# Router columns merged into expert 0's gate product, and the expert ranking moved and spread over VectorE

## What is computed

```python
logits = x @ router_w                          # (256, 32)
scores = sigmoid(logits)
grouped = (scores + router_bias).reshape(T, 8, 4)
group_scores = top_k(grouped, 2).sum(-1)
masked = grouped in the 4 best groups, else 0
top_k_index = top_k(masked, 8)
tkw = scores[top_k_index] / sum * 2.5
routed = sum over the 8 experts of tkw * ((silu(x @ w_gate) * (x @ w_up)) @ w_down)
shared = (silu(x @ sw_gate) * (x @ sw_up)) @ sw_down     # hidden width 512
return routed + shared
```

## Time and profile before

| | us |
|---|---|
| median of 3 runs | 532.67 |
| lowest and highest run | 532.51, 533.3 |
| the profiled execution | 532.38 |
| span of that execution | 530.3 |
| TensorE busy (matmuls) | 520.7 |
| VectorE busy | 389.1 |
| ScalarE busy | 304.3 |
| GpSimd busy | 29.4 |

### The profile page before, as it was taken

One profiled execution on the slowest core, in us unless ns is written; L12 is line 12 of the kernel. 1 busy time (PEld: TensorE's weight loads), 2 busy tenths in 40 slices (PEclk: granted clock), 3 DMA queues, 4 the chain that ended last, 5 costly groups with the idle time before them and its releaser, 6 DMA issues.

```text
span 530.3 us, 9657 instructions
## 1 busy us (share of the span) xinstructions
PE 520.7 (98%) x3454; PEld 469.0 (88%) x3454; DVE 389.1 (73%) x616; ACT 304.3 (57%) x470; POOL 29.4 (6%) x48
## 2 busy tenths in 40 slices
PE   9999999999989999989999999999999999999997
PEld 7988888888669989879989999999999999999997
DVE  6777555557788988776987777768677776767675
ACT  5665587753476776637546465554646465554631
POOL 1000000000632131010000000000000000000000
PEclk9999999999999999999999999999999999999999
DMA  8775624455412232516355646464554646455521
GB/s 286 289 231 175 209 99 155 162 159 157 127 35 78 86 136 90 199 41 237 121 183 173 203 157 222 143 225 163 193 189 167 204 161 223 146 215 171 185 71 40
DMA packets 19459, 86.24 MB, mean 163 GB/s; under 512 B 2160, under 2 KB 2416, under 8 KB 19312
## 3 DMA queue, kind: packets, MB, share of 16 engines
q1 hardware_dynamic: 19440, 85.99, 47.9%
HBM read 85.46 MB, written 0.52 MB: 162 GB/s over the span
## 4 chain that ended last, share of the span: by engine, by line
PE 92%; DVE 5%; ACT 2%; issue 1%; POOL 0%; ACTq 0%; DVEq 0%; POOLq 0%
PE bank L936 33%; PE bank L429 16%; PE bank L433 16%; PE bank L432 16%; PE bank L437 2%; PE bank L501 1%; PE bank L438 1%; PE bank L439 1%; PE bank L573 1%; DVE w_lo L282 1%; PE bank L715 1%; PE bank L735 1%; PE bank L696 1%; ACT operands L305 1%; PE bank L455 1%
## 5 line engine op out<-in xcount | busy, mean ns | idle before, releaser
L277 ACT CAST w_hi<-raw 128x768 fp32r<-128x768 f32 (+3 forms) x158 | 158.9, 1040 | 96.6 <-PE bank L936 82.8
L282 DVE TENSOR_TENSOR w_lo<-raw,w_hi 128x1280 fp32r<-128x1280 f32 (+3 forms) x156 | 182.7, 1213 | 13.5 <-ACT w_hi L277 11.4
L429 PE MATMUL bank<-w_hi,operands 128*128 128x512 f32 (+1 forms) x322 | 126.1, 392 | 1.2 <-DVE operands L330 1.0
L433 PE MATMUL bank<-w_hi,operands 128*128 128x512 f32 (+1 forms) x322 | 124.0, 385 | 0.0
L432 PE MATMUL bank<-w_lo,operands 128*128 128x512 f32 (+1 forms) x322 | 123.8, 385 | 0.0
L936 PE MATMUL bank<-xt_hi,w_lo 128*128 128x256 f32 x512 | 108.6, 283 | 0.0
L936 PE MATMUL bank<-xt_hi,w_hi 128*128 128x256 f32 x512 | 108.4, 283 | 0.0
L936 PE MATMUL bank<-xt_lo,w_hi 128*128 128x256 f32 x512 | 108.3, 283 | 0.0
L936 PEld LDWEIGHTS bank<-xt_hi,w_hi 128*128 128x128 f32 x512 | 83.7, 190 | 2.6
L936 PEld LDWEIGHTS bank<-xt_hi,w_lo 128*128 128x128 f32 x512 | 81.7, 190 | 0.0
L936 PEld LDWEIGHTS bank<-xt_lo,w_hi 128*128 128x128 f32 x512 | 81.7, 190 | 0.0
(11 more groups left out here) (182 smaller groups left out, 565.4 us busy)
## 6 DMA issues: line engine op xcount, KB each, us to landing
raw<-w_exp_dram SPq DMA_DIRECT2D x34, 896.0 KB, 4.7
raw<-w_exp_dram SPq DMA_DIRECT2D x34, 640.0 KB, 5.6
raw<-ctx_t_dram SPq DMA_DIRECT2D x16, 512.0 KB, 4.6
raw<-ctx_n_dram SPq DMA_DIRECT2D x16, 512.0 KB, 4.1
raw<-w_mla_dram SPq DMA_DIRECT2D x8, 512.0 KB, 3.6
raw<-w_mla_dram SPq DMA_DIRECT2D x8, 448.0 KB, 3.9
raw<-wq_dram SPq DMA_DIRECT2D x4, 256.0 KB, 5.4
raw<-wk_dram SPq DMA_DIRECT2D x2, 512.0 KB, 7.3
```

The source lines that it names most:

```text
L277: act.copy(w_hi[:, t.slot, at:at + n], raw[:, t.slot, at:at + n]).then_inc(hi_split[k], 1)
L282: eng.tensor_tensor(w_lo[:, t.slot, at:at + n], raw[:, t.slot, at:at + n], w_hi[:, t.slot, at:at + n].bitcast(F32), ALU.subtract) \
L429: ins = pe.matmul(o, a[0], b[0], start=start, stop=False)
L433: return pe.matmul(o, a[1], b[0], start=False, stop=stop)
```

## The change

It takes the router's columns from `smalls` and stores them behind each chunk of expert 0's gate columns in a separate array `w_first` (piece 0 of expert 0 grows from 1280 to 1408 columns, the slot from 3072 to 3200). Expert 0's gate product has 288 columns instead of 256, the last 32 being logits, tokens down. Its up product goes to bank 2 + h. ScalarE copies the logits out and takes the sigmoid of 128 x 64 values, with no transposes. TensorE, ScalarE and VectorE get new orders. The router's own split, matmuls and score transposes go. `expert_lo(2)`, which stood behind `expert_add(1)`, now stands inside the ranking, and `expert_add(0)` behind it. The core of the diff, first SyncE and TensorE (in the code `expert_add(0, s)` and the like with j = 0 are expert s; with j = 1, expert 2 + s):

```diff
+FIRST_SIZES = (1408, 1024, 768)
...
+            load(Tile(0, T_E), w_first, FIRST_SIZES)
+            load(Tile(0, T_E + 1), w_exp[0], E_SIZES)
...
+            def first_gate(h, split, told=None):
+                t = Tile(0, T_E)
+                n = I + E
+                for c in range(NC):
...
+                    ins = product(bank[4 + 2 * h][:, 0:n], (xt_hi[:, c, half(h)], xt_lo[:, c, half(h)]),
+                                  wcols(t, c * n, n), c == 0, c == NC - 1, told if c == 0 else None)
+                ins.then_inc(bank_full[4 + 2 * h], 1)
...
-            expert_rows(0, 0, 4, told=used[1], split=V_LN3)
-            expert_rows(1, 0, 5, midway=lambda: transpose_half(xn, 1, 0, xn_ready, 6))
-            expert_rows(0, 1, 6, split=V_LN3 + 2)
-            expert_rows(1, 1, 7, told=used[2])
-            transpose_hidden(0)
+            first_gate(0, V_LN3, told=used[1])
+            first_up(0)
+            second_rows(0, midway=lambda: transpose_half(xn, 1, 0, xn_ready, 6))
+            first_gate(1, V_LN3 + 2)
+            first_up(1)
+            second_rows(1, told=used[2], midway=lambda: transpose_hidden(0))
...
-            pe.wait_ge(rw_split, 1)
-            for c in range(NC):
-                ins = product(bank[6][0:E, 0:T], (rw_hi[:, c, :], rw_lo[:, c, :]),
-                              (xt_hi[:, c, :], xt_lo[:, c, :]), c == 0, c == NC - 1)
-            ins.then_inc(bank_full[6], 1)
-            transpose_hidden(1)
-            down(0, 0, told=used[2])
-            pe.wait_ge(ev_lo, V_H + 1)
-            pe.wait_ge(sigmoid_ready, 1)
-            for h in range(2):
-                ins = pe.transpose(bank[7][:, h * E:h * E + E], score_t[:, half(h)], ident[0:E, 0:E])
-            ins.then_inc(bank_full[7], 1)
+            pe.wait_ge(logits_copied, 2)
+            down(0, 0, told=used[2])
+            transpose_hidden(1)
             gate_up(0, 2, told=used[1])
-            pe.wait_ge(score_taken, 1)
             down(0, 1, told=used[2])
```

ScalarE's order:

```diff
             rows_silu(1, 0)
             rows_silu(0, 1)
+            for h in range(2):
+                act.copy(logits[:, h * E:h * E + E], bank[4 + 2 * h][:, I:I + E]).then_inc(logits_copied, 1)
             split_hi(act, Tile(0, T_E + 2), 0, E_SIZES)
+            out_hi(act, 2, F23["h_t"], h_hi[:, 0, :], 512)
             rows_silu(1, 1)
...
+            split_hi(act, Tile(0, T_E + 2), 2, E_SIZES)
+            act.wait_ge(logits_copied, 2)
+            act.activation(score, logits, ACT.Sigmoid).then_inc(sigmoid_ready, 1)
+            out_hi(act, 3, F23["h_t"], h_hi[:, 1, :], 512)
             split_hi(act, Tile(0, T_E + 3), 0, E_SIZES)
```

VectorE's order; the `out_lo` of bank 3 stands behind line 1632, the splits of expert 3 behind line 1653:

```diff
             rows_hidden(0, 1)
+            out_lo(dve, 2, V_H, h_hi[:, 0, :], h_lo[:, 0, :], 512)
             split_lo(dve, Tile(0, T_E + 2), 0, E_SIZES)
             rows_hidden(1, 1)
-            out_lo(dve, 0, V_H, h_hi[:, 0, :], h_lo[:, 0, :], 512)
             split_lo(dve, Tile(0, T_E + 2), 2, E_SIZES)
-            out_lo(dve, 1, V_H + 1, h_hi[:, 1, :], h_lo[:, 1, :], 512)
...
-            dve.wait_ge(bank_full[7], F7["score"])
-            dve.tensor_copy(score, bank[7][:, 0:2 * E]).then_inc(score_taken, 1)
-            for k in (0, 2):
-                split_lo(dve, Tile(0, T_E + 3), k, E_SIZES)
-            split_lo(dve, Tile(0, T_E + 2), 1, E_SIZES)
-            expert_add(0, 0)
+            dve.wait_ge(sigmoid_ready, 1)
...
-            expert_product(1, 0)
+            out_lo(dve, 3, V_H + 1, h_hi[:, 1, :], h_lo[:, 1, :], 512)
...
+            for k in (0, 2):
+                split_lo(dve, Tile(0, T_E + 3), k, E_SIZES)
+            split_lo(dve, Tile(0, T_E + 2), 1, E_SIZES)
+            expert_product(1, 0)
             for h in range(2):
                 m = masked[:, h * E:h * E + E]
                 then(dve.max(top8[:, h * TOP:h * TOP + TOP], m))
                 then(dve.match_replace(replaced[:, h * E:h * E + E], top8[:, h * TOP:h * TOP + TOP], m, TAKEN))
+            expert_lo(1, 0)
+            expert_add(0, 0)
             then(dve.tensor_tensor(picked, replaced, masked, ALU.not_equal))
...
             expert_add(0, 1)
-            expert_lo(1, 0)
             expert_splits(1, 0)
             expert_add(1, 0)
```

More of the change, by code:

```diff
@@ L60 @@
 T_E = T_M + PAIRS
-OFF = (0, 1280, 2304)
-SLOT = 3072
+OFF = (0, 1408, 2432)
+SLOT = 3200
 X_SIZES = (1024, 1024)
@@ L68 @@
 E_SIZES = (1280, 1024, 768)
-C_MASK, C_COS, C_SIN, C_RW, C_BIAS, C_GQ, C_GKV, C_TIE = 0, 256, 512, 768, 896, 960, 1152, 1280
+FIRST_SIZES = (1408, 1024, 768)
+C_MASK, C_COS, C_SIN, C_BIAS, C_GQ, C_GKV, C_TIE = 0, 256, 512, 768, 832, 1024, 1152
 C_END = C_TIE + 2 * GROUPS * GROUPS
-F01 = dict(ln1=1, s_even=2, s_new=6, pt_even=7, ot=11, ln2=12, rope=13, y=14, ln3=15, h_t=16, moe=16)
-F23 = dict(q=1, s_odd=2, pt_new=6, pt_odd=7, ot=11, qkv=12, rope=13, scores=14, pt=15, ln3=30, moe=30)
+F01 = dict(ln1=1, s_even=2, s_new=6, pt_even=7, ot=11, ln2=12, rope=13, y=14, ln3=15, moe=15)
+F23 = dict(q=1, s_odd=2, pt_new=6, pt_odd=7, ot=11, qkv=12, rope=13, scores=14, pt=15, ln3=30, up=31, h_t=32, moe=32)
 F45 = dict(ln1=1, k=2, v=3, wo=4, ln2=5, c=6)
@@ L81 @@
 F67 = dict(pv=1, c=2, rows=11)
-F6 = dict(v=3, router=12, moe=13)
-F7 = dict(qk=3, score=12, moe=13)
+F6 = dict(v=3, moe=12)
+F7 = dict(qk=3, moe=12)
 V_LN1, V_Q, V_K, V_V, V_PT, V_OT, V_LN2, V_C, V_M0 = 1, 5, 7, 9, 11, 29, 33, 37, 41
@@ L108, in free, with perceiver_layer @@
         return self.number - 1 if k < 2 else self.number + (-1 - T_E)
-def perceiver_layer(nc, x, small, wq, wk, wv, wo, ctx_t, ctx_n, w_qkv, w_rope, w_mla, w_exp, out):
+def perceiver_layer(nc, x, small, wq, wk, wv, wo, ctx_t, ctx_n, w_qkv, w_rope, w_mla, w_first, w_exp, out):
     with ExitStack() as ctx:
@@ L212, in perceiver_layer @@
         h_row = scores[:, 1, 1024:2048].rearrange("p (r n) -> p r n", r=2)
-        score_t = scores[0:E, 1, 3200:3200 + T]
         def route(at, n):
             return scores[:, 1, 2048 + at:2048 + at + n]
+        logits, score = route(1152, 2 * E), route(0, 2 * E)
         x_loaded = [sem(f"x_loaded{h}") for h in range(2)]
@@ L409, in _ @@
                     load(Tile(j, T_M + s), w_mla[bass.ds(j * 2 + s, 1)].squeeze(0), M_SIZES)
-            for s in range(2):
-                load(Tile(0, T_E + s), w_exp[s], E_SIZES)
+            load(Tile(0, T_E), w_first, FIRST_SIZES)
+            load(Tile(0, T_E + 1), w_exp[0], E_SIZES)
             with sp.Fori(0, NE // 2 - 1) as j:
                 for s in range(2, 4):
-                    load(Tile(j, T_E + s), w_exp[bass.ds(j * 2 + s, 1)].squeeze(0), E_SIZES)
+                    load(Tile(j, T_E + s), w_exp[bass.ds(j * 2 + (s - 1), 1)].squeeze(0), E_SIZES)
             for k, (h, at, n) in enumerate(((0, 0, 512), (1, 0, 256), (1, 256, 256))):
@@ L892, in _, with first_up, second_rows @@
             out_pair(last, last=True, halves=(1,), heads=(1,))
-            def expert_rows(s, h, b, told=None, split=None, midway=None):
-                t = Tile(0, T_E + s)
+            def first_gate(h, split, told=None):
+                t = Tile(0, T_E)
+                n = I + E
+                for c in range(NC):
+                    if h == c == 0:
+                        ready(t, 0)
+                    if c % 2 == 0:
+                        pe.wait_ge(ev_lo, split + c // 2)
+                    ins = product(bank[4 + 2 * h][:, 0:n], (xt_hi[:, c, half(h)], xt_lo[:, c, half(h)]),
+                                  wcols(t, c * n, n), c == 0, c == NC - 1, told if c == 0 else None)
+                ins.then_inc(bank_full[4 + 2 * h], 1)
+            def first_up(h):
+                t = Tile(0, T_E)
+                for c in range(NC):
+                    if h == 0 and c == 1:
+                        ready(t, 2)
+                    at = OFF[2] + (c - 1) * I if c else NC * (I + E)
+                    ins = product(bank[2 + h][:, 0:I], (xt_hi[:, c, half(h)], xt_lo[:, c, half(h)]),
+                                  wcols(t, at, I), c == 0, c == NC - 1)
+                    if h == 1 and c == 0:
+                        ins.then_inc(used[0], 1)
+                ins.then_inc(bank_full[2 + h], 1)
+            def second_rows(h, told=None, midway=None):
+                t = Tile(0, T_E + 1)
                 for u in range(2):
@@ L903, in expert_rows @@
                             ready(t, k)
-                        if split is not None and u == 0 and c % 2 == 0:
-                            pe.wait_ge(ev_lo, split + c // 2)
                         at = (u * NC + c) * I if k == 0 else OFF[2] + (c - 1) * I
-                        ins = product(bank[b][:, u * I:u * I + I], (xt_hi[:, c, half(h)], xt_lo[:, c, half(h)]),
+                        ins = product(bank[5 + 2 * h][:, u * I:u * I + I], (xt_hi[:, c, half(h)], xt_lo[:, c, half(h)]),
                                       wcols(t, at, I), c == 0, c == NC - 1, told if u == c == 0 else None)
@@ L1167, in _ @@
                 pair_step(j, 2)
[L1168 removed]
+            pair_step(0, PAIRS - 3, FIRST_SIZES)
```

(7 more changed lines are left out.)

43 lines of the change are left out of this document (15 added, 28 removed).

## The result

| | before | after |
|---|---|---|
| median of all 10 runs of each, taken in turn | 532.9 | 534.52 |
| lowest and highest run | 532.51, 533.3 | 533.45, 535.42 |
| the profiled execution | 532.38 | 533.45 |
| span of that execution | 530.3 | 531.7 |

The ratio is 1.0028, 95% interval 1.002 to 1.0036. The change makes the kernel slower by 1.6 us by the medians (1.5 by the ratio), where I had forecast 533.0 and no change that can be measured; 534.52 also lies above the upper end of my range, 534.2.

The account below looks back on a forecast made before the run. TensorE bounds the kernel, but VectorE has no reserve from 260.50 to 269.55: gate_up(3) starts 1.41 us earlier, yet a new 2.0 us wait makes gate_up(4) about 0.3 later. 532.38 + 0.3 = 532.7, by the median 533.0; range 531.6 to 534.2.

Parts of the forecast that it names:

- What bounds: From 278 us TensorE alone sets the time; from 260.50 to 269.55 VectorE has no reserve, busy 8.50 of 9.05 us.
- the sum from 240.81 to gate_up(4): Experts: gate_up(3) starts 1.41 us earlier, at 259.12; piece 0 of expert 4 is ready 10.49 later; about +0.3 at gate_up(4).
- the price of 288 columns: Expert 0's gate product: each matmul takes 0.1337 us, on a line between 0.120 for 256 columns and 0.229 for 512.
- the wait of some 0.2 at down(0): TensorE before down(0): a new wait of 0.1 us for the low part of the turned hidden values.
- VectorE's 2.5 us of idle time: VectorE before expert_lo(2): idle 2.4 us, 259.8 to 262.17, until ScalarE has written the high part.
- the wait of 1.93 us: TensorE before gate_up(4): stands 2.0 us until VectorE has split expert 4's piece 0.
- The 128 more columns of piece 0: zero: Head pairs: about 0.1 us each on ScalarE and VectorE, covered, so zero; 0.2 if the cover were gone.
- The clock falls in the new wait: Slower rival: the 2.0 us wait brings the slow pace back for gate_up(4), 3 us or more, 536; chance 0.03.
- The sum is 532.38 + 0.3: Total: 532.7 for an execution like the profiled one, which was 0.29 below the median, so 533.0.
- The gain survives: Faster rival: expert 4's piece 0 is split by 267.6, so -1.94 us, 530.7 by the median; chance 0.11.
- gate_up(3) comes later: Slower rival: time lost between 240.81 and 259.12, at down(0) behind ScalarE's cast, reaches the end, 534.2; chance 0.10.

Follow-up runs that it names:

- the trace with 12 additions: Kernel before with 12 additions of 128x128 on VectorE in front of the splits that hold expert 4's piece 0; 538.27 us, ratio 1.01.
- the one with the split moved: Changed kernel with only VectorE's split of expert 0's piece 0 moved behind the step of the next head pair; 533.21 us, ratio 1.0007.
- The two repairs: Changed kernel with expert_lo(2) back behind expert_add(1), 531.33 us; the same with VectorE's split of expert 0's piece 0 behind the next head pair's step, 530.74.
- the best version: Changed kernel with expert_lo(2) back behind expert_add(1) and VectorE's split of expert 0's piece 0 behind the next head pair's step; 530.74 us, ratio 0.9959.

## Why the prediction was wrong, step by step

**What bounds, and the sum from 240.81 to gate_up(4): right.** TensorE's times, the price of 288 columns (243.41 - 241.82 = 1.59 for 12, so 0.133 each, forecast 0.134), the wait of some 0.2 at down(0) (forecast 0.1), VectorE's 2.5 us of idle time (2.4), the wait of 1.93 us (2.0): all as worked out, to 0.1. In the Trainium skill, TensorE: Matmul & The Clock Gate, section Back-to-back issue gap, the isolated gap between two matmuls at full clock is N / 2.4 + 2.5 ns, which gives an estimate of 122.5 for 288 columns; the measured 133 decides, and the line between this kernel's own 256 and 512 columns was nearer. gate_up(4) and what follows loses 0.38 us (an offset of 1.01 at 241.82 and of 276.71 - 275.32 = 1.39 at down(3)) where I had +0.3.

**"The 128 more columns of piece 0: zero": wrong, +0.46 us.** This is the first step that failed. I costed the columns at nothing because TensorE's busy tenths stand at 9 among the head pairs. A tenth of 9 in slices of 13 us hides a wait of 0.5 us, and above all it says nothing of slack: it does not tell whether the next thing on TensorE waits for VectorE. The row to read was VectorE's queue: which instruction stands behind this split, and who waits for it. I had also priced 0.1 each for ScalarE and VectorE in case the cover was gone, and left out the transfer ahead of them, which with 0.39 in the two traces shown, and 0.21 by the means of five, was the largest of the three.

**"The clock falls in the new wait": chance 0.03, and it happened in 12 of 16 executions.** This is the second. I had forecast the wait, 2.0 us, and named what it could do; against it I had only that the clock held in the stretch with the wait of before, which was 0.25 us. A short wait is no evidence for a long one, and the longest of that trace behind the start, 1.25 us at 158.94, is none either. The size was off the other way. I took the pace of the kernel's first matmuls for a whole gate_up and wrote 3 us or more. At the low clock two matmuls of 256 columns do take 0.43 us (275.15 to 275.58 in the trace with 12 additions) instead of 0.24, but the low stretch ends after 3.4 us and holds 14 to 19 matmul records, not 48: it costs 1.2 to 1.5 by the traces. Between the medians of the two kinds of executions lie 0.8 us in the changed kernel (534.63 against 533.79) and 1.1 in the one with the split moved.

**"The sum is 532.38 + 0.3":** two small terms were missing. The device time less the span is 2.05 to 2.06 us in the seven traces with the arrangement of before and 1.79 to 1.81 in the five that hold the change, 0.26 less. I did not look for the reason. And the profiled execution was not 0.29 below the median, as by the runs shown, but 0.42 to 0.52 below the medians of the four longer sets of runs (532.80 to 532.90).

**Together.** 532.86 + 0.46 + 0.38 - 0.26 = 533.4 for the changed kernel at full clock; its four runs lie at 533.45 to 533.83, median 533.79. With 1.2 to 1.5 for the clock it is 534.6 to 534.9 for the others, measured 534.14 to 535.42. The two repairs come out of the same terms. With the low part moved back gate_up(4) to down(3) is 1.82 us earlier against the stretch's end than before, so 532.86 + 0.46 - 1.82 - 0.26 = 531.24 (measured 531.33); with the split moved as well, 0.22 below the price of before instead of 0.46 above it, 530.56 (530.74). Up to 0.4 us of a total stays unexplained, less than the times of the kernel before scatter (532.33 to 533.66).

**The rivals.** "The gain survives", 530.7, has the time of the best version, in part by luck: that version also moves the split of expert 0's piece 0, of which the rival says nothing, and with the low part alone moved back it is 531.33. In its mechanism the rival was right about the repair: what it needed was expert 4's piece 0 split in time, and moving one line gives that. I had seen that VectorE would arrive "2.4 us too soon anyway" and took it as a reason why nothing could be gained, when it was the reserve. "gate_up(3) comes later" gave 534.2, near the measured time and by another mechanism: the 0.46 us were lost before 240.81, not after it.

## What to carry to other kernels

When an operation grows in a stage that seems full or idle by its share, read what stands behind it in the same engine's queue and who waits for that, and count transfer, cast and split in series. In a queue in fixed order put the work that waits for another engine behind the work that doesn't: two such moves (one line each) turned +1.6 us into -2.1. And if a forecast puts a new wait on TensorE, look in the trace for a wait of that length; if there is none, the clock after it is an open cost with a real chance.

## What the runs showed of the hardware

The granted clock of TensorE after a wait amid full work went down in none of 5 executions at 1.29 us, in 20 of 33 at 1.92 to 1.95 (12 of 16, 5 of 12, 3 of 5 by kernel), in 4 of 4 at 3.25. It then stood at 0.50 for 3.4 us although TensorE had work again; with the wait of 1.92 us the fall came 1.6 us after the restart, with 1.95 us 0.5 after it, with 3.25 us 0.3 before it. Shorter waits that every trace has, of 0.96 and 1.25 us, brought no fall in any of the twelve. The same program thus has two groups of times some 1 us apart, and a single trace shows one of them.

The same 60 matmuls of an expert took 8.470 and 8.480 us in the two kernels with slots 120 and 96 columns longer, and 8.503 in the others: the 256-column ones were faster, the 512-column ones slower. That is 0.7 to 1 us over the experts of this kernel, as much as a fall of the clock. That the place of the tiles in memory does it is likely, but no run shows it.
